# Rows and probabilities turned through VectorE and DRAM instead of on TensorE, in a two-block layer kernel on one core

## The reference

```python
xn = _layernorm(x, axis=-1)
s = _L0_attn_ref(xn, ...)      # xn + rmsnorm(y @ W_out.T) * norm_w; the state starts at zero,
                               # so y is one weighted factor per channel times xn @ W_in.T
g = _silu(_L0_ffn_ref(xn, W1, W2, W3))
x = x + s * g
xn = _layernorm(x, axis=-1)
s = _L1_attn_ref(xn, qkv, o_proj, gamma, beta)
g = _silu(_L1_ffn_ref(xn, W1, W2, W3))
x = x + s * g

# the ffn: hidden = fwht(silu(xn @ W1.T) * (xn @ W3.T)); out = hidden @ W2.T   (H = 1024)
# the attention of block 1:
x_norm = (x - mu) / jnp.sqrt(var + 1e-05) * gamma + beta
q, k, v = (x_norm @ qkv[:, i * 256:(i + 1) * 256] for i in (0, 1, 2))
scores = where(causal, q @ k.T / 16, -inf)
out = softmax(scores) @ v @ o_proj + x        # x here is the xn of the block
```

## Time and profile before

| | |
|---|---|
| time, median of 3 runs | 383.63 us (382.83 to 383.70) |
| the profiled execution | 383.55 us |
| its span | 381.8 us |
| TensorE busy | 374.7 us, 98% |
| VectorE busy | 235.4 us, 62% |
| ScalarE busy | 158.3 us, 41% |
| GpSimd busy | 87.6 us, 23% |
| mean granted clock of TensorE | 0.994 |

### The profile page before, as it was taken

The page is one execution under the profiler, slowest core; times in us unless marked ns, Lnnn a source line. Parts: engine busy times, 40 slices in busy tenths (PEclk is TensorE's granted clock), DMA queues, the critical chain, the costliest instruction groups (busy, mean ns, idle before and its releaser), DMA issues.

```text
span 381.8 us, 5244 instructions
## 1 busy us (share of the span) xinstructions
PE 374.7 (98%) x1961; PEld 319.3 (84%) x1961; DVE 235.4 (62%) x469; ACT 158.3 (41%) x311; POOL 87.6 (23%) x111
## 2 busy tenths in 40 slices
PE   6999999999999999999999999999999999999996
PEld 3888888878888888888988988888888888888885
DVE  5589973596358736785457954479443795334832
ACT  2654451444135512551374513644236352354410
POOL 1143510153013201266304220024200152000302
PEclk9899999999999999999999999999999999999999
DMA  7993000120012001000010000101001010010101
GB/s 229 296 356 107 2 1 7 47 86 2 0 49 91 1 0 44 14 3 0 21 36 1 2 0 14 43 0 57 0 8 47 3 57 0 2 48 7 57 0 55
DMA packets 21248, 17.08 MB, mean 45 GB/s; under 512 B 5092, under 2 KB 20712, under 8 KB 21224
## 3 DMA queue, kind: packets, MB, share of 16 engines
q1 hardware_dynamic: 21224, 16.76, 14.3%
HBM read 10.98 MB, written 2.10 MB: 34 GB/s over the span
## 4 chain that ended last, share of the span: by engine, by line
PE 94%; DVE 3%; DMA 1%; SPq 1%; issue 0%; ACT 0%; DVEq 0%
PE GU L257 18%; PE GU L259 18%; PE GU L258 18%; PE O L257 9%; PE O L259 8%; PE O L258 8%; PE T L264 5%; PE GU L264 1%; DMA stage<-in_L_ffn_W 1%; PE O L264 1%; PE O L333 1%; PE T L257 1%; PE T L258 1%; PE T L259 1%; DVE hf L796 1%; DVE hid L717 1%
## 5 line engine op out<-in xcount | busy, mean ns | idle before, releaser
L606 ACT ACTIVATE hf<-GU 128x512 f32<-128x512 f32 x64 | 38.2, 598 | 87.7 <-DVE hid L717 51.0
L796 DVE TENSOR_TENSOR hf<-hf,GU 128x512 f32<-128x512 f32 x64 | 43.9, 685 | 48.1 <-PE GU L259 41.7
L257 PE MATMUL GU<-XT,W1T 128*128 128x512 f32 x128 | 51.3, 400 | 0.0
L257 PE MATMUL O<-hid,W2hi 128*128 128x512 f32 (+1 forms) x128 | 50.2, 392 | 0.0
L259 PE MATMUL GU<-XT,W1T 128*128 128x512 f32 x128 | 50.0, 391 | 0.0
L258 PE MATMUL GU<-XT,W1T 128*128 128x512 f32 x128 | 50.0, 390 | 0.0
L257 PE MATMUL GU<-XT,W3T 128*128 128x512 f32 x128 | 49.9, 390 | 0.0
L259 PE MATMUL GU<-XT,W3T 128*128 128x512 f32 x128 | 49.9, 390 | 0.0
L258 PE MATMUL GU<-XT,W3T 128*128 128x512 f32 x128 | 49.8, 389 | 0.0
L259 PE MATMUL O<-hid,W2lo 128*128 128x512 f32 (+1 forms) x128 | 49.1, 384 | 0.0
L258 PE MATMUL O<-hid,W2hi 128*128 128x512 f32 (+1 forms) x128 | 49.1, 383 | 0.0
(11 more groups left out here) (187 smaller groups left out, 706.6 us busy)
## 6 DMA issues: line engine op xcount, KB each, us to landing
stage<-in_L_ffn_W SPq DMA_DIRECT2D x24, 256.0 KB, 4.9
sT<-GX SPq DMA_DIRECT2D x112, 32.0 KB, 1.9
X<-in_L_attn_x SPq DMA_DIRECT2D x1, 1536.0 KB, 9.1
out<-X SPq DMA_DIRECT2D x3, 512.0 KB, 2.9
wqkv<-in_L_attn_qkv SPq DMA_DIRECT2D x1, 768.0 KB
X<-in_L_attn_x SPq DMA_DIRECT2D x2, 256.0 KB, 2.9
win<-in_L_attn_W_in SPq DMA_DIRECT2D x1, 512.0 KB
wout<-in_L_attn_W_out SPq DMA_DIRECT2D x1, 512.0 KB
```

The costliest lines, as they stand in the source:

```text
L257: pe.matmul(o, lhs(0), rhs(0), start=start, stop=False)
L606: act.activation(hf[:, c % 2, :], GU[:, c % 2, 0, :], ACT.Silu).then_inc(silu_done, 1)
L796: dve.tensor_tensor(hf[:, c % 2, :], hf[:, c % 2, :], GU[:, c % 2, 1, :], ALU.mult).then_inc(mul_done, 1)
```

## The change

`x_transposes` goes, but for the first group, and so do the z transposes and those of P. Each is replaced by a path like the gate's. VectorE turns 32x32 blocks (`x_turn` of the rows into GX, `p_turn` of the exponentials into PX). SP writes the result to DRAM in one DMA (`scatter`) and reads it back in four that put each block to its partitions (`gather`); both the gate and the x rows use GX and sT, by turns, and waits keep them apart. ScalarE makes the high halves from SBUF, and the low halves of x and P are made by GpSimd.

z is taken from the turned x: in columns, the factor of a row is the same on all partitions. `spread_c2` writes c2 to a line in DRAM in 4-byte elements and loads it back broadcast to 128 partitions (c2B). VectorE's `scale_z` multiplies, ScalarE applies gamma and beta, then come the high half and GpSimd's low half, in tiles of their own (zfull, ZT).

In block 1 the work between VectorE's chunks is earlier: statistics after chunk 0, gate product after 1, normalise and the turn after 4. GpSimd's `second_norm` stands ahead of `add_to_x`. `move_gate` now takes one DMA to DRAM and four back. `p_turn` stands ahead of the low halves of v.

```diff
+            def scatter(scratch, done):
+
+                sp.dma_start(scratch.rearrange("j p f -> p j f"), GX[:, :, :, :, :].rearrange("p j t k a -> p j (t k a)")).then_inc(done, 16)
+
+            def gather(scratch, done):
+
+                for j in range(QUADS):
+                    sp.dma_start(turned[j * Q:(j + 1) * Q].rearrange("p i t k a -> p i (t k a)"),
+                                 scratch[j].rearrange("(i b) f -> b i f", i=QUADS)).then_inc(done, 16)
+
             def move_gate(n):
 
                 sp.wait_ge(gate_flipped, 2 * n + 2)
-                for i in range(QUADS):
-                    for j in range(QUADS):
-                        sp.dma_start(gate_rows[j * Q:(j + 1) * Q, i, :, :, :].rearrange("p t k a -> p (t k a)"),
-                                     GX[i * Q:(i + 1) * Q, j, :, :, :].rearrange("p t k a -> p (t k a)")).then_inc(gate_moved, 16)
+                scatter(swap_gate, gate_out)
+                sp.wait_ge(gate_out, 16 * n + 16)
+                gather(swap_gate, gate_moved)
+
+            def move_rows(n):
+
+                sp.wait_ge(rows_turned, 2 * n)
+                scatter(swap_rows, rows_out)
+                sp.wait_ge(rows_out, 16 * n)
+                gather(swap_rows, rows_moved)
+
+            def move_p(n):
+
+                m = n - NB
+                sp.wait_ge(p_turned, 2 * m + 2)
+                sp.dma_start(swap_p.rearrange("j p f -> p j f"), PX[:, :, :, :].rearrange("p j c b -> p j (c b)")).then_inc(p_out, 16)
+                sp.wait_ge(p_out, 16 * m + 16)
+                for j in range(QUADS):
+                    sp.dma_start(PL[j * Q:(j + 1) * Q].rearrange("p q c b -> p q (c b)"),
+                                 swap_p[j].rearrange("(q a) f -> a q f", q=QUADS)).then_inc(p_moved, 16)
+
+            def spread_c2(m):
+
+                sp.wait_ge(c2_ready, m + 1)
+                sp.dma_start(c2_line.rearrange("(t p) -> p t", p=P), c2[:, :], allow_slow_non_contiguous=True).then_inc(c2_out, 16)
+                sp.wait_ge(c2_out, 16 * m + 16)
+                if m == 0:
+                    sp.wait_ge(up_done, NB * HC)
+                sp.dma_start(c2B[:, :], c2_line.rearrange("(a r) -> a r", a=1).broadcast_to([P, ROWS])).then_inc(c2_in, 16)
...
+            move_rows(1)
             for n in range(1, NB):
                 move_gate(n - 1)
                 if n < 3:
                     sp.wait_ge(w_tr, 2 * PAIRS + 2 * n)
                     sp.wait_ge(w2_tr, PAIRS + n)
                     load_pair(1, n + 1, stage[:, (n + 1) % 2, :, :], stage_loaded[(n + 1) % 2])
+                move_rows(n + 1)
+            spread_c2(0)
             move_gate(NB - 1)
+            move_p(NB)
+            spread_c2(1)
+            move_rows(NB + 1)
...
+                n = NB + 1 + b
+                move_gate(n - 1)
+                move_p(n)
+                if b < NB - 2:
+                    spread_c2(b + 2)
                 sp.wait_ge(combined, TILES * b + TILES * (NB + 1))
                 sp.dma_start(out_dram[:, bass.ds(b * TILES, TILES), :], X[:, bass.ds(b * TILES, TILES), :]).then_inc(out_stored, 16)
+                if b < NB - 2:
+                    move_rows(n + 1)
...
             def block0_group(n):
-                x_transposes(n)
...
-                if prev_layer == 1:
-                    pe.wait_ge(pt_ready, 3 * m)
-                x_transposes(n)
                 if prev_layer == 0:
                     pe.wait_ge(u_ready, 2 * PAIRS)
-                for i in range(2):
-                    down_chunk(prev_layer, n - 1, i)
-                pe.wait_ge(z_ready, m + 1)
-                pe.wait_ge(mul_done, 8 * n)
-                for k in range(KC):
-                    transposes(GU[:, 1, k, :], [PZ[:, t * D + k * P:t * D + (k + 1) * P] for t in range(TILES)]).then_inc(zt_tr, 1)
-                for i in range(2, 6):
+                for i in range(6):
                     down_chunk(prev_layer, n - 1, i)
                 pe.wait_ge(zt_ready, 2 * m + 2)
...
-                    if c == HC - 3:
-                        pe.wait_ge(v_ready, 2 * m + 2)
-                        for b in range(3):
-                            transposes((T[:, 0, :], T[:, 1, :], O[:, 0, :])[b],
-                                       [PZ[:, q * P:(q + 1) * P] for q in range(4 * b, min(4 * b + 4, BLOCKS))]).then_inc(pt_tr, 1)
+                pe.wait_ge(v_ready, 2 * m + 2)
...
+            def x_hi(n):
+
+                act.wait_ge(up_done, 8 * n)
+                if n <= NB:
+                    act.wait_ge(mix_done, 2 * n)
+                act.wait_ge(rows_moved, 64 * n)
+                for k in range(KC):
+                    act.activation(xT[0][k].rearrange("p (t q b) -> p t q b", t=TILES, q=QUADS),
+                                   rows_at[:, :, k, :].rearrange("p q (t b) -> p t q b", t=TILES), ACT.Copy).then_inc(xt_hi, 1)
 
             def gate(n):
 
+                act.wait_ge(xt_ready, 2 * n + 4)
+                if n >= NB - 1:
+                    act.wait_ge(z_scaled, 2 * (n - NB) + 4)
...
-                    hi(zT[0][k], sT[:, k, :], zfull_ready, 2 * m + k + 1, zt_hi)
+                    act.wait_ge(z_scaled, 2 * m + k + 1)
+                    act.activation(zfull[:, k, :], zfull[:, k, :], ACT.Identity, scale=gb[:, 0, k:k + 1], bias=gb[:, 1, k:k + 1]).then_inc(zfull_ready, 1)
+                for k in range(KC):
+                    hi(zT[0][k], zfull[:, k, :], zfull_ready, 2 * m + k + 1, zt_hi)
...
+                    if c == 4:
+                        act.wait_ge(p_moved, 64 * m + 64)
                         for b in range(3):
-                            lo_, hi_ = 4 * b * P, min(4 * b + 4, BLOCKS) * P
-                            bank = (T[:, 0, :], T[:, 1, :], O[:, 0, :])[b]
-                            hi(ZP[:, 0, lo_:hi_], bank[:, 0:hi_ - lo_], pt_tr, 3 * m + b + 1, pt_hi)
+                            c0, c1 = 4 * b, min(4 * b + 4, BLOCKS)
+                            act.activation(blocks_of(0, c0, c1), PL[:, :, c0:c1, :].rearrange("p q c b -> p c q b"), ACT.Copy).then_inc(pt_hi, 1)
...
+            def x_turn(n):
+
+                dve.wait_ge(xn_ready, n + 1)
+                if n > 1:
+                    dve.wait_ge(gate_out, 16 * (n - 1))
+                for k in range(KC):
+                    dve.transpose(rows_gx[:, :, k, :].rearrange("p j (t b) -> p t j b", t=TILES),
+                                  rows2[n % 2][:, :, k * P:(k + 1) * P].rearrange("p t (j a) -> p t j a", j=QUADS)).then_inc(rows_turned, 1)
+
+            def scale_z(n):
+
+                m = n - NB
+                dve.wait_ge(c2_in, 16 * m + 16)
+                dve.wait_ge(rows_moved, 64 * n)
+                for k in range(KC):
+                    dve.tensor_tensor(zfull[:, k, :].rearrange("p (t q b) -> p t q b", t=TILES, q=QUADS),
+                                      rows_at[:, :, k, :].rearrange("p q (t b) -> p t q b", t=TILES),
+                                      c2B[:, :].rearrange("p (t q b) -> p t q b", t=TILES, q=QUADS), ALU.mult).then_inc(z_scaled, 1)
...
+                dve.wait_ge(rows_out, 16 * n + 16)
...
+                if c == (4 if n < NB else 1):
...
-                if c == 1 and not last:
+                if c == (1 if n < NB else 0) and not last:
                     stats(n + 1, ((n + 1) % NB) * TILES)
-                if c == 6 and not last:
+                if c == (6 if n < NB else 4) and not last:
                     dve.wait_ge(combined, 4 * n)
                     normalise(n + 1, ((n + 1) % NB) * TILES)
+                    x_turn(n + 1)
...
+                if m:
+                    dve.wait_ge(p_out, 16 * m)
+                for h, (c0, c1) in enumerate(((0, block_at(TILES - 1)), (block_at(TILES - 1), BLOCKS))):
+                    dve.wait_ge(exp_done, 4 * m + 3 + h)
+                    dve.transpose(PX[:, :, c0:c1, :].rearrange("p j c b -> p c j b"),
+                                  PZ[:, c0 * P:c1 * P].rearrange("p (c j a) -> p c j a", j=QUADS, a=Q)).then_inc(p_turned, 1)
...
+                    recurrent_scale(n - 1)
+                    scale_z(n)
                 else:
                     attention_scale(n - 1)
-                dve.wait_ge(prod_ready, 4 * n - 4)
-                for k in range(KC):
-                    dve.wait_ge(zt_tr, 2 * m + k + 1)
-                    dve.tensor_scalar(sT[:, k, :], GU[:, 1, k, :], gb[:, 0, k:k + 1], gb[:, 1, k:k + 1], ALU.mult, ALU.add)\
-                       .then_inc(zfull_ready, 1)
-                if prev_layer == 0:
-                    recurrent_scale(n - 1)
-                else:
-                    x_lo(n)
...
+            def x_lo(n):
+                for k in range(KC):
+                    pool.wait_ge(xt_hi, 2 * n + k + 1)
+                    pool.tensor_tensor(xT[1][k].rearrange("p (t q b) -> p t q b", t=TILES, q=QUADS), rows_at[:, :, k, :].rearrange("p q (t b) -> p t q b", t=TILES),
```

(11 more changed lines are left out.)

81 lines of the change are left out of this document (41 added, 40 removed).

## The result

The changed kernel takes 391.2 us against 383.66 before, median of four runs each; the ratio is 1.019, interval 1.017 to 1.021. It is 1.9% slower. (One of its four runs took 1279.62 us, which nothing here explains; the median of the other three is 390.9.) The profiled execution has a span of 389.1 us against 381.8, which is 7.3 us more.

What follows compares the result with a forecast made beforehand. TensorE, busy for 98% of the span, was taken to bound the kernel; -13.9 + 0.6 + 6.1 + 1.7 + 7.5 + 2.5 = +4.5 on 383.55 gave 388.1 us, range 375 to 396.

Steps and rivals of the forecast that it cites:

- a) transposes: TensorE, all groups: 128 transposes of x, z and P leave, 0.109 us each, -13.9 us.
- b) head: Head: x_turn(1) on VectorE ahead of mult 6 of group 0 delays TensorE, +0.6 us, ends 0 and 1.4.
- c) entry: Entry of block 1: TensorE waits for group 4's z through DRAM exchange, factors and broadcast, +6.1 us, ends 5 and 10.
- d) clock: Behind the entry's wait: TensorE works at half clock for a stretch, +1.7 us (0 to 1.7).
- e) collision: Up chunk 4, groups 4 to 6: VectorE's normalise and GpSimd's low halves of P take turns, +7.5 us, ends 0 and 10.
- 378.1: Total in us if only the entry waits and normalise and P's low halves do not hold each other up; chance 0.29.
- f) clock behind it: Behind the three 2.5 us stalls of groups 4 to 6: even chance of 1.7 us lost each, +2.5 us (0 to 5.1).
- Cover, z of groups 5 to 7: Groups 5 to 7: low half of z ready near 274, TensorE wants it near 277; hidden with 2.9 us to spare.
- Rival B: Only the entry of block 1 waits; the VectorE and GpSimd collision and its clock loss vanish, 378.1 us; chance 0.29.
- C (all hidden): Rival: z arrives in time at the entry too, so all waits but the head's are hidden, 370.3 us; chance 0.13.

Runs made afterwards that it cites:

- the second experiment: Changed kernel with ScalarE making the high halves of P behind its chunk 5 instead of 4, GpSimd's low halves following; 396.48 us.
- the first experiment: Changed kernel with group 4's factors worked out right behind its rstd and their line sent ahead of the rows' scatter; 384.35 us.
- the two kernels with the early line: Changed kernel with group 4's factor line ahead of the rows' scatter, 384.35 us; the same plus P's halves behind chunk 5 and X's store behind the gathers, 380.23 us.
- the best kernel: Changed kernel with P's halves behind chunk 5, late store, group 4's z on TensorE, and groups 5 to 7's factors turned behind chunk 3, in pieces; 371.81 us.

## Why the prediction was right, and where it was not

The forecast was 388.1 us, range 375 to 396, and slower likelier than faster; measured were 391.2. Four of the terms came by the mechanism that was given for them: the transposes, the entry, the clock behind it and the collision. Their sizes were off, one term didn't come at all, and errors of opposite sign hid each other.

- **a) transposes, -13.9.** Held. 0.102 each by the doubled transposes, and the span's sum closes to within 0.6 us with 0.109.
- **b) head, +0.6: about 0.2.** From TensorE's first up matmul to the transposes of group 1's rows 39.32 us passed before (12.02 to 51.34), and to the down chunks, which stand in their place now, 39.49 (11.30 to 50.79). The kernels of the experiments with this head have 39.47 to 39.55. The mechanism held and hid more than I took: x_turn took 1.30, the low half of the hidden chunk behind it rose from 1.16 to 2.32 beside GpSimd's sum, and the sum of U fell from 3.42 to 1.21. The 0.2 are a part of the 0.6 that the span's sum left open. That the whole head began 0.7 us earlier is not the change's doing.
- **c) entry, +6.1 with ends 5 and 10: measured 13.2.** The failed step is the line of factors: I took 2.0 us "by the smallest issues", and it took 7.8. The nearest row by bytes was the wrong neighbour; by the runs with pieces what counts is the number of elements, and no row of before had 4-byte ones. I wrote that no row shows it, and then let the upper end of the range, 10, be four landings 1 us longer each, so at most 3.0 for the line. The broadcast was 4.4 instead of 2.6, by a row that was not a broadcast. The other links were within 1 us: scatter 2.8 for 3.0, gathers 2.5 for 2.0 (off the chain: the line left when they were issued), engines 5.3 for 5.4. The two together are 7.6 us too much, and 7.1 was missing.
- **d) clock, +1.7: 2.9.** The mechanism held, the size was taken from the head's 3.4 us stretch, and here the lower level lasted 5.8 us from the first matmul on.
- **e) collision, +7.5: 5.2, and 4.9 by itself.** The rule of the Trainium skill, "SBUF — State Buffer", "Who interferes with whom", decided rightly between this case and 378.1. The trace agrees: three of VectorE's four operations each ended 0.15 us behind one of GpSimd's, while a product with one input in SBUF kept 0.65 beside GpSimd (271.02 in the second experiment). The term was too large because VectorE's low half at chunk 3 was hardly held up: it kept 0.68 (265.72), so only normalise was stretched, and both were over after 4.4 us (270.08) instead of my 5.1 (255.23 to 260.3).
- **f) clock behind it, +2.5: nothing.** The stalls were 1.60 to 1.96 us instead of 2.5, and the granted clock of the windows around them was 1.00. In the experiments an even chance fits: of the four stalls of 2 to 3 us in running work half clock came with those of 2.21 and 3.00, some 1.7 us lost in each, and not with those of 2.44 and 2.73. So the length of a stall alone doesn't decide it.
  The Trainium skill, "TensorE: Matmul & The Clock Gate", Part 1, ties the half clock to an engine gone idle, and that reading gave 0 here. The trace agrees for these three stalls; the 2.21 and the 3.00 of the experiments it would not have given.
- **Cover, z of groups 5 to 7, 2.9 to spare.** In the changed kernel GpSimd was done at 286.0 and TensorE wanted z at 286.73: 0.7 to spare, and only because it had lost 1.6 to 2.0 in the same group. Without that it was 1.3 to 2.4 us late (second experiment). The failed step is one that I never made: the queue behind spread_c2 has the store of X and then the scatter, and I priced each transfer as if it were alone.

Terms c and d came 8.3 us above the prediction, b, e and f together 5.2 below (0.4, 2.3 and 2.5). That the time lies only 3 us from the forecast is luck in part: with c and d at their measured sizes and nothing else changed, the same sum would have given 396.4, just outside the range.

Rival B (only the entry waits) and C (all hidden) did not come as the change stands; with the entry's and the collision's cause taken away and the factors sent in pieces, the kernel is at 371.8, which is 0.6 over C's 370.3 plus 0.9 for the eight transposes that stayed. So the premise, that what was moved can be covered, was right for all but group 4's z; it needed another order.

## What to carry to other kernels

Work taken off the engine that bounds a kernel is worth its length only after the new path has been walked link by link, and a small transfer is not a cheap one: here 2 KB in 512 elements took 7.8 us and 512 KB in pieces of 1 KB 2.8. Make factors contiguous first, send them early, and keep them from going out right ahead of a large transfer that something waits for. When a stall is removed and the kernel gets slower, look for the next chain that it covered. An edit must be judged in its place: the same piece-wise line cost 3.6 us behind the turn and gained 2.1 ahead of it.

## What the runs showed of the hardware

- 2 KB in 512 elements of 4 bytes, SBUF to DRAM, land after 7.6 to 9.0 us over all kernels, also with nothing ahead of them (8.9 at 152.54 in the first experiment); the same bytes in 16 pieces by four DMAs took 2.7 us behind the gathers at the entry and 2.1 to 2.2 elsewhere.
- A broadcast of 2 KB to 128 partitions (256 KB) lands after 4.3 to 5.2 us right behind a line of 4-byte elements, after 3.5 to 3.6 where that line had landed well before (the two kernels with the early line), and after 3.0 to 3.6 behind pieces. Why it depends on that was not tried.
- A scatter of 512 KB lands after 2.8 to 2.9 us alone, 5.8 to 6.2 with a broadcast 0.4 us ahead of it that follows a line of 4-byte elements, 4.5 with one that follows pieces, 7.1 with a store of 512 KB between broadcast and scatter.
- TensorE's clock stayed full behind stalls of 1.60, 1.96, 2.44 and 2.73 us. It went to half for 3.4 us with stalls of 2.21 and 3.00 (some 1 us after work had begun again in the first, just ahead of it in the second), and behind 4.4 to 13.9 us of idleness the work began at half clock and stayed there for 3.5 to 5.8 us. What decides it was not settled.
- VectorE's four tensor_scalar operations took 1.38 alone and 3.76 beside three GpSimd operations of 3.6 us in all, in the changed kernel and in the best kernel with P's halves behind chunk 4. The 32x32 transposes and a product with one input in PSUM kept their 0.65 to 0.71 beside GpSimd (269.79 and 271.02 in the second experiment), and a low half with both inputs in SBUF took 1.77 for 0.68.
